# Four additions over all nodes leave GpSimd: bias rows and residual on VectorE, the last two layers' biases as rounded rows in TensorE's sums

## The chip, the core and the metric

The kernel runs on one core of a Trainium2 chip. The metric is the device time in microseconds of one execution, as the median of several; lower is better.

## What is computed

Four graph networks follow each other over 625 nodes with 512 numbers each and 10,000 edges. Each takes the normed and rectified nodes and is added to them:

```python
h = jnp.maximum(_layernorm(x, axis=-1), 0.0)
x = x + L0(h, ...)   # x = h + attention(h) @ Wo + bo;  x + gelu(norm(x) @ W1 + b1) @ W2 + b2
h = jnp.maximum(_layernorm(x, axis=-1), 0.0)
x = x + L1(h, ...)   # edge filters, segment sums
h = jnp.maximum(_layernorm(x, axis=-1), 0.0)
x = x + L2(h, ...)   # three layers: own part and two means over neighbours
h = jnp.maximum(_layernorm(x, axis=-1), 0.0)
x = x + L3(h, ...)   # two layers: agg + x @ root + bias
```

Four of the additions are the matter of the change: the row `bo` on the residual of L0's attention, the row `b2` and the residual on `x`, and the bias rows of L3's two layers (`bias1`, `bias2`).

## The kernel before

Nodes lie in 5 chunks (`NC`) of 128 partitions. `xs` holds x and `hn` the normed nodes, each 128 x 5 x 512 fp32 in SBUF. `rows` holds two rows of 512, spread over all partitions: first `bo` and `b2`, later, loaded into the same place, `bias1` and `bias2`. The program is written out by hand, one instruction stream an engine, with semaphores between them; nothing is scheduled by a planner, so the order in the code is the order on each engine.

The stretches that matter, in order of time:

- **Sorting and V (to 170 us).** GpSimd scatters the edges by 80 indirect DMAs (L736), and then gathers the logits by 84 (L749), while VectorE and ScalarE copy the dense products (L1319). VectorE then adds the row `bv` to V's five chunks (L1325) as TensorE finishes them.
- **Softmax and messages (to 460 us).** VectorE combines L3's basis matrices (`combine_run`), then makes the softmax. GpSimd gathers V for 84 tiles of edges into a ring of 21 (`gather_v`, L758). After the first 21 it adds `bo` to `hn` (L764), then goes on as VectorE frees ring entries.
- **Norm 2 (462 to 500 us).** For each chunk m, TensorE gives the product with Wo, VectorE adds it to `hn[m]` and takes mean and variance (`add_wo`, L1460, then L1281 to L1283), ScalarE the square root (L851), VectorE the factors (L1288, L1289), ScalarE the normed nodes (L856, `s_norm`), TensorE transposes them, ScalarE copies them twice, as rounded upper part `hT_r` and whole `h2_all` (L963, L964), and VectorE subtracts (`rest_of_norm2`, L1467, `s_h2_rest`).
- **FFN1 (to 596 us).** 32 blocks through one PSUM bank, each of 12 fp32r matmuls, emptied by ScalarE with Gelu (L996). Block n of the first chunk half waits for `s_h2_rest` of 3 chunks. From the fifth block on, counting matmuls lie between them.
- **L2 and L3 (from 900 us).** Each fp32 product is three fp32r matmuls: upper x upper, upper x rest, rest x upper (`three`, L2138). A layer is `own` (the nodes' own part into five banks), then for two sides i `side` (products G, emptied by ScalarE twice, L1079 and L1080, and subtracted by VectorE, L1651) and `neighbours` (their sum over the adjacency), which needs all five chunks of G. Meanwhile VectorE combines L3's basis matrices (`combine`, L1675).

GpSimd's queue after the gathers is: wait for norm 2 of all chunks, two additions over all nodes (L768, L769), then the loads for a first combination (`load_lead`, L778). VectorE waits for `s_added` of these before it goes on in FFN1 (L1520) and writes into `hn`. In the last layer (l = 4) GpSimd adds `bias2` to `xs` (L821) between the loads of two weights, and VectorE waits for it before the last additions (L1739). `bias1` is put into `own` of l = 3 by an fp32 matmul of one row:

```python
if l == 3:
    pe.wait_ge(s_l3par, 6 * 16)
    pe.matmul(o, ones[0:1, :], rows[0:1, 0, :], start=True, stop=False)
```

Of the kernel before, what the change touches and what calls it, by code (L numbers as in the profile page):

```python
# [26 lines left out]
ALU = mybir.AluOpType  # L27
# [3 lines left out]
P = 128  # L31
# [64 lines left out]
def seen(turn, m=NC - 1):  # L96

    return sum(NC if t in EACH else 1 for t in range(turn)) + (m + 1 if turn in EACH else 1)
# [81 lines left out]
def build(nc, a, out):  # L180

    with ExitStack() as ctx:
        def sb(name, shape, dt=F32):
            return ctx.enter_context(nc.sbuf_tensor(name, shape, dt))
# [122 lines left out]
        rows = sb("rows", [P, 2, D])  # L307
# [201 lines left out]
        bas_run = [work[:, at:at + 1024] for at in (2048, 3072, 4096)]  # L509
        bas = [aux[:, 8448:9472], aux[:, 9472:10496], wA[:, 6400:7424]]  # L510
# [46 lines left out]
        def _(sp):  # L557
# [45 lines left out]
            for j, count in enumerate((3, 3, 2, 2)):  # L603
                sp.wait_ge(s_pair_out[j], 16 * count)
            sp.dma_start(wo, a["L0_gnn_Wo"].rearrange("(k p) n -> p k n", p=P)).then_inc(s_wo, 16)
# [93 lines left out]
        def _(pool):  # L699
# [61 lines left out]
            gather_v(range(RING))  # L761
            pool.wait_ge(s_norm, seen(1))
            pool.wait_ge(s_wo, 3 * 16)
            pool.tensor_tensor(hn[:, :, :], hn[:, :, :], rows[:, 0, :].unsqueeze(1).to_broadcast([P, NC, D]), ALU.add).then_inc(s_added, 1)  # L764
            gather_v(range(RING, NT))

            pool.wait_ge(s_norm, seen(2))
            step(pool.tensor_tensor(xs[:, :, :], xs[:, :, :], hn[:, :, :], ALU.add))  # L768
            pool.tensor_tensor(xs[:, :, :], xs[:, :, :], rows[:, 1, :].unsqueeze(1).to_broadcast([P, NC, D]), ALU.add).then_inc(s_added, 1)  # L769

# [43 lines left out]
            for l in range(1, LAYERS):  # L814
# [3 lines left out]
                if l == LAYERS - 1:  # L818
                    pool.wait_ge(s_norm, seen(5))
                    pool.wait_ge(s_l3par, 6 * 16)  # L820
                    pool.tensor_tensor(xs[:, :, :], xs[:, :, :], rows[:, 1, :].unsqueeze(1).to_broadcast([P, NC, D]), ALU.add).then_inc(s_added, 1)  # L821
# [333 lines left out]
        def _(dve):  # L1155
# [165 lines left out]
            step(dve.memset(hot[:, NT:NT + 4, :], 0.0))  # L1321
            dve.wait_ge(s_wqkv, 32)
# [125 lines left out]
            dve.wait_ge(s_added, 1)  # L1448
# [9 lines left out]
            def add_wo(m):  # L1458
                dve.wait_ge(s_job, plan.number(f"wo{m}", 0))
                step(dve.tensor_tensor(hn[:, m, :], plan.slot(ps, f"wo{m}", 0), hn[:, m, :], ALU.add))  # L1460
                dve.nop().then_inc(s_by_dve, 1)
                moments(2, m, hn)

# [56 lines left out]
            dve.wait_ge(s_added, 2)  # L1520
# [174 lines left out]
            for l in range(LAYERS):  # L1695
# [21 lines left out]
                if l == 0:  # L1717
                    dve.wait_ge(s_w_upper, 3)
                    dve.tensor_tensor(gws_r[:, 1, :], gw[:, :, :, :].rearrange("p l r k -> p (l r k)"), gws_r[:, 0, :], ALU.subtract)
                rest_of_weight(l, 2)  # L1720
# [18 lines left out]
            dve.wait_ge(s_added, 3)  # L1739
# [5 lines left out]
        def _(pe):  # L1745
# [409 lines left out]
            def own(l, m):  # L2155

                if m == 0:
                    pe.wait_ge(s_w_rest, 3 * l + 1)
                pe.wait_ge(s_rest, 15 * l + m + 1)
                o = ps[:, D * m:D * (m + 1)]  # L2160
                if l == 3:
                    pe.wait_ge(s_l3par, 6 * 16)
                    pe.matmul(o, ones[0:1, :], rows[0:1, 0, :], start=True, stop=False)
                for k in range(K4):
                    last = three(o, h_upper[:, m, cols(k)], h_rest[:, m, cols(k)], w_upper[0][:, k, :], w_rest[0][:, k, :], start=k == 0 and l != 3)
                if m == NC - 1:
                    last.then_inc(s_w_used, 1)
# [98 lines left out]
```

## Time and profile before

| | before |
|---|---|
| median of 3 runs | 1398.02 us (1396.14, 1398.02, 1404.21) |
| the profiled execution, its own time | 1396.14 us |
| its span, first to last instruction | 1394.4 us |
| mean granted TensorE clock | 0.918 of 2.4 GHz |
| TensorE busy | 1173.3 us, 84% |
| VectorE busy | 870.1 us, 62% |
| ScalarE busy | 436.0 us, 31% |
| GpSimd busy | 442.2 us, 32% |

Times in rows are microseconds from the span's start. PE is TensorE's matmul, PEld its weight load, DVE VectorE, ACT ScalarE, POOL GpSimd; L12 is line 12 of the kernel before. An fp32 matmul shows as two records, and a matmul's record is longer than its share of TensorE, since they are pipelined; the distance of starts tells the pace. Idle time in brackets, with what ended it, stands before the instruction that it belongs to.

### The profile page before, as it was taken

How to read it: one execution, taken by the hardware profiler on the slowest of the kernel's cores; microseconds unless marked ns; L12 is line 12 of the kernel's file. 1: busy time of each engine (PE TensorE's matmuls, PEld its weight loads, DVE VectorE, ACT ScalarE, POOL GpSimd, SP SyncE). 2: the span in 40 equal slices, each digit the busy share in tenths (PEclk: the TensorE clock that was granted, in tenths of full speed). 3: DMA queues.
4: the chain of work that ended last, by engine and by line, in shares of the span. 5: the costliest groups of instructions: out<-in, count | busy, mean ns of one | idle time of the engine just before them, and what ended most of it. 6: DMA issues, size and time to landing. Idle time of an engine off the chain costs nothing.

```text
span 1394.4 us, 15192 instructions
## 1 busy us (share of the span) xinstructions
PE 1173.3 (84%) x5432; PEld 822.4 (59%) x5433; DVE 870.1 (62%) x1392; ACT 436.0 (31%) x617; POOL 442.2 (32%) x408
## 2 busy tenths in 40 slices
PE   4597678058798759999997999799799998989996
PEld 4464344033353347744464999567588786778885
DVE  7618326883475557979368997646769877583211
ACT  2315122011211532110053996634232324333220
POOL 5777577783477030111007772000000000010000
PEclk8798889578899979999978999999899999899898
DMA  6216899873766013452016110204645656323001
GB/s 216 45 13 211 278 380 360 277 217 128 242 181 185 17 40 112 136 170 87 31 57 157 49 47 15 91 31 165 206 132 195 206 175 206 108 72 109 0 0 37
DMA packets 74832, 187.83 MB, mean 135 GB/s; under 512 B 14918, under 2 KB 17963, under 8 KB 69524
## 3 DMA queue, kind: packets, MB, share of 16 engines
q1 hardware_dynamic: 45540, 100.35, 21.2%
q0 software_dynamic: 21600, 64.66, 16.1%
q10 hardware_dynamic: 7632, 22.02, 4.2%
q8 instruction: 38, 0.62, 0.2%
q14 instruction: 22, 0.18, 0.0%
HBM read 149.93 MB, written 36.97 MB: 134 GB/s over the span
## 4 chain that ended last, share of the span: by engine, by line
PE 57%; DVE 17%; DMA 10%; issue 6%; ACT 5%; POOL 2%; SPq 2%; DVEq 0%; ACTq 0%; PEldq 0%
PE ps L2138 22%; DMA work<-in_L_gnn_basis 5%; PE ps L2043 5%; PE ps L2101 4%; PE ps L2033 4%; PE ps L1954 4%; DVE aux L1675 3%; PE ps L1810 3%; PE ps L1868 2%; DVE work L1352 2%; PE ps L2013 2%; POOL aux L758 2%; PE ps L1841 2%; PE ps L2086 1%; DMA xs<-in_x 1%
## 5 line engine op out<-in xcount | busy, mean ns | idle before, releaser
L2138 PE MATMUL ps<-work_r,hT_r 128*128 128x512 f32 x600 | 194.8, 406 | 2.1 <-DVE att_r L1647 1.4
L2138 PEld LDWEIGHTS ps<-work_r,hT_r 128*128 128x128 f32 x600 | 114.2, 193 | 32.8 <-issue 4.7
L2138 PE MATMUL ps<-work_r,att_r 128*128 128x512 f32 x300 | 120.8, 403 | 0.0
L736 POOL DMA_INDIRECT etab_d<-aux,edge x80 | 95.2, 1190 | 49.7 <-issue 48.6
L1651 DVE TENSOR_TENSOR bT_r<-bT,fT_r 128x512 fp32r<-128x512 f32 x50 | 38.7, 774 | 107.3 <-ACT fT_r L1080 107.3
L1675 DVE SCALAR_TENSOR_TENSOR aux<-aux,attb 128x1024 f32<-128x1024 f32 x84 | 103.1, 1278 | 2.2 <-DMA aux<-in_L_gnn_basis 2.2
L1810 PE MATMUL ps<-wA 128*128 128x512 f32 x192 | 89.0, 624 | 13.4 <-DMA wA<-in_L_gnn_W_bwd 6.6
L749 POOL DMA_INDIRECT lg<-pair_d,reli x84 | 87.2, 1038 | 29.1 <-issue 25.3
L2138 PE MATMUL ps<-fT_r,wA_r 128*128 128x512 f32 x250 | 87.1, 417 | 10.6 <-DVE bT_r L1651 10.6
L1954 PE MATMUL ps<-work,hT_r 128*128 128x512 f32 x168 | 86.2, 646 | 10.0 <-DVE work L1426 5.7
L1352 DVE SCALAR_TENSOR_TENSOR work<-work,attb 128x1024 f32<-128x1024 f32 x58 | 72.0, 1299 | 28.5 <-DMA work<-in_L_gnn_basis 28.5
L1493 DVE TENSOR_SCALAR work<-iota,srcf,flag 128x640 bf16<-128x640 f16 x168 | 64.4, 448 | 40.6 <-PE ps L2014 40.6
L758 POOL DMA_INDIRECT aux<-v_d,srcx x64 | 80.6, 1260 | 20.0 <-issue 18.0
L2138 PE MATMUL ps<-fT_r,aux_r 128*128 128x512 f32 x250 | 80.8, 401 | 3.6 <-DVE bT_r L1651 3.6
L2101 PE MATMUL ps<-work_r 128*128 128x256 f32 x280 | 70.6, 289 | 9.8 <-DVE wA_r L1581 9.8
L1810 PEld LDWEIGHTS ps<-wA 128*128 128x128 f32 x192 | 37.9, 200 | 61.5 <-issue 51.1
L2043 PE MATMUL ps<-wA,aux 128*128 128x512 f32 x160 | 73.1, 599 | 1.2 <-issue 1.2
L799 POOL DMA_DIRECT2D work<-early_d x9 | 4.9, 544 | 207.8 <-PE ps L2138 135.1
L2101 PE MATMUL ps<-wA_r,work_r 128*128 128x256 f32 x280 | 69.3, 288 | 0.0
L2138 PEld LDWEIGHTS ps<-work_r,att_r 128*128 128x128 f32 x300 | 57.8, 193 | 14.2
L2138 PEld LDWEIGHTS ps<-fT_r,wA_r 128*128 128x128 f32 x250 | 49.2, 197 | 25.9 <-DVE bT_r L1651 12.4
L1426 DVE TENSOR_TENSOR work<-aux,lg 128x512 f32<-128x512 f32 x64 | 44.3, 693 | 28.5 <-DMA aux<-v_d,srcx 16.0
(387 smaller groups left out, 2646.0 us busy)
## 6 DMA issues: line engine op xcount, KB each, us to landing
aux<-in_L_gnn_basis SPq DMA_DIRECT2D x44, 512.0 KB, 3.9
work<-in_L_gnn_basis SPq DMA_DIRECT2D x30, 512.0 KB, 7.6
fT<-in_L_gnn_basis POOLq DMA_DIRECT2D x24, 512.0 KB, 4.4
wA<-in_L_gnn_basis SPq DMA_DIRECT2D x22, 512.0 KB, 3.9
work<-early_d POOLq DMA_DIRECT2D x9, 1024.0 KB, 6.5
wA<-in_L_gnn_W_self ACTq DMA_DIRECT2D x7, 1024.0 KB, 14.9
pair_d<-aux SPq DMA_DIRECT2D x5, 1280.0 KB, 13.7
early_d<-work ACTq DMA_DIRECT2D x5, 1024.0 KB, 17.0
```

What stands on the lines that cost most here:

```text
L736: pool.indirect_dma_start(out=etab_d, out_offset=bass.IndirectOffsetOnAxis(ap=row[:, t:t + 1], axis=0), in_=etab[:, t, :], in_offset=None) ...
L749: pool.indirect_dma_start(out=lg[:, t, :], out_offset=None, in_=pair_d, in_offset=bass.IndirectOffsetOnAxis(ap=reli[:, t:t + 1], axis=0)). ...
L758: pool.indirect_dma_start(out=ring[t % RING], out_offset=None, in_=v_d, in_offset=bass.IndirectOffsetOnAxis(ap=srcx[:, t:t + 1], axis=0)). ...
L1352: ins = dve.scalar_tensor_tensor(acc_run[:, r], bas_run[b % 3], factor, acc_run[:, r], ALU.mult, ALU.add)
L1493: last = dve.tensor_scalar(hotS[:, 4 * k + j, :], iota16[:, :], srcf[:, at], flag[:, r, at], ALU.is_equal, ALU.mult)
L1675: ins = dve.scalar_tensor_tensor(acc[:, r], bas[u], factor, acc[:, r], ALU.mult, ALU.add)
L1810: last = pe.matmul(to[:, k], w[:, o, k * P:(k + 1) * P], early_s[:, o, :], start=o == 0, stop=o == K4 - 1)
L1954: pe.matmul(ps[:, bass.ds(c * 512, D)], one, msg[:, j, :], start=False, stop=False, skip_group_check=True)\
L2033: last = pe.matmul(o, w, h[:, k, nodes], start=k == i == 0, stop=(k, i) == (K4 - 1, 2))
L2043: last = pe.matmul(plan.slot(ps, "ffn2", m), node(g1T, j, m), w2s[:, j, :], start=j == 0, stop=j == 15)
L2101: last = pe.matmul(ps[:, 512 * m:512 * m + NF], hotL[k][:, j, m * P:(m + 1) * P], part[:, 4 * k + j, :], start=False, stop=False)
L2138: last = pe.matmul(o, lhsT, rhs, start=start and n == 0, stop=stop and n == 2)
```

## The change

On GpSimd the four additions go, and with them the waits ahead of them. `bo` and `b2` are now added by VectorE, both over all nodes, behind the copies of the dense products and before the additions to V. The residual `xs += hn` is split into five, one behind each chunk's `moments` in `add_wo`. `bias1` and `bias2` become two-partition fp32r rows, the rounded row and what it lacks, made once by VectorE in layer 0; TensorE adds them in `own` of l = 3 and l = 4 with one fp32r matmul of two rows each. SP's one added wait is met long before.

```diff
-        rows = sb("rows", [P, 2, D])
+        rows, rows_r = sb_twice("rows", [P, 2, D])
...
+        bias_upper = wA_r[0:2, 7424:7424 + D]
+        ones_r = wA_r[0:2, 7936:7936 + P]
...
+            sp.wait_ge(s_wo, 32)
             sp.dma_start(wo, a["L0_gnn_Wo"].rearrange("(k p) n -> p k n", p=P)).then_inc(s_wo, 16)
...
-            gather_v(range(RING))
-            pool.wait_ge(s_norm, seen(1))
-            pool.wait_ge(s_wo, 3 * 16)
-            pool.tensor_tensor(hn[:, :, :], hn[:, :, :], rows[:, 0, :].unsqueeze(1).to_broadcast([P, NC, D]), ALU.add).then_inc(s_added, 1)
-            gather_v(range(RING, NT))
-
+            gather_v(range(NT))
             pool.wait_ge(s_norm, seen(2))
-            step(pool.tensor_tensor(xs[:, :, :], xs[:, :, :], hn[:, :, :], ALU.add))
-            pool.tensor_tensor(xs[:, :, :], xs[:, :, :], rows[:, 1, :].unsqueeze(1).to_broadcast([P, NC, D]), ALU.add).then_inc(s_added, 1)
...
-                if l == LAYERS - 1:
-                    pool.wait_ge(s_norm, seen(5))
-                    pool.wait_ge(s_l3par, 6 * 16)
-                    pool.tensor_tensor(xs[:, :, :], xs[:, :, :], rows[:, 1, :].unsqueeze(1).to_broadcast([P, NC, D]), ALU.add).then_inc(s_added, 1)
...
             step(dve.memset(hot[:, NT:NT + 4, :], 0.0))
+            dve.wait_ge(s_wo, 32)
+            dve.wait_ge(s_norm, seen(1))
+            for j, nodes in enumerate((hn, xs)):
+                dve.tensor_tensor(nodes[:, :, :], nodes[:, :, :], rows[:, j, :].unsqueeze(1).to_broadcast([P, NC, D]), ALU.add).then_inc(s_added, 1)
...
-            dve.wait_ge(s_added, 1)
+            dve.wait_ge(s_added, 2)
...
                 moments(2, m, hn)
+                dve.tensor_tensor(xs[:, m, :], xs[:, m, :], hn[:, m, :], ALU.add).then_inc(s_added, 1)
...
-            dve.wait_ge(s_added, 2)
+            dve.wait_ge(s_added, 2 + NC)
...
+                    dve.wait_ge(s_l3par, 6 * 16)
+                    step(dve.tensor_copy(ones_r, ones[0:2, :]))
+                    for j in range(2):
+                        step(dve.tensor_copy(bias_upper, rows[0:2, j, :]))
+                        step(dve.tensor_tensor(rows_r[0:2, j, :], rows[0:2, j, :], bias_upper, ALU.subtract))
+                        step(dve.tensor_copy(rows_r[0:1, j, :], bias_upper[0:1]))
...
-            dve.wait_ge(s_added, 3)
...
-                if l == 3:
-                    pe.wait_ge(s_l3par, 6 * 16)
-                    pe.matmul(o, ones[0:1, :], rows[0:1, 0, :], start=True, stop=False)
+                if l >= 3:
+                    pe.matmul(o, ones_r, rows_r[0:2, l - 3, :], start=True, stop=False)
                 for k in range(K4):
-                    last = three(o, h_upper[:, m, cols(k)], h_rest[:, m, cols(k)], w_upper[0][:, k, :], w_rest[0][:, k, :], start=k == 0 and l != 3)
+                    last = three(o, h_upper[:, m, cols(k)], h_rest[:, m, cols(k)], w_upper[0][:, k, :], w_rest[0][:, k, :], start=k == 0 and l < 3)
```

On VectorE, between the clearing of the last four tiles of `hot` and the additions to V (`aux<-ps,wA`), the order before is:

```order
148 L1321 MEMSET work 128x256
149 L1325 TENSOR_TENSOR aux<-ps,wA 128x512 [waits s_pre_job,s_wqkv,s_dve]
150 L1325 TENSOR_TENSOR aux<-ps,wA 128x512 [waits s_pre_job] x4
151 L1330 CAST srcx<-att 128x28 [waits s_att0]
152 L1331 CAST dstx<-att 128x28
```

and now:

```order
148 L1312 MEMSET work 128x256
149 L1316 TENSOR_TENSOR hn<-hn,rows 128x2560 [waits s_norm,s_wo,s_dve]
150 L1316 TENSOR_TENSOR xs<-xs,rows 128x2560
151 L1320 TENSOR_TENSOR aux<-ps,wA 128x512 [waits s_pre_job,s_wqkv]
152 L1320 TENSOR_TENSOR aux<-ps,wA 128x512 [waits s_pre_job] x4
```

The two additions over all nodes stand ahead of the first addition to V.

On VectorE in norm 2, for chunk 1 and the beginning of chunk 2, the order before is (the subtraction into `wA_r` is that of a W1 block):

```order
363 L1460 TENSOR_TENSOR hn<-ps,hn 128x512 [waits s_job]
364 L1281 BN_STATS bst<-hn 128x6 [waits s_dve]
365 L1282 BN_AGGR mv<-bst 128x2 [waits s_dve]
366 L1283 TENSOR_SCALAR var<-mv 128x1 [waits s_dve]
367 L1288 RECIPROCAL rstd<-std 128x1 [waits s_std]
368 L1289 SCALAR_TENSOR_TENSOR nmr<-mv,rstd 128x1 [waits s_dve]
369 L1444 TENSOR_TENSOR wA_r<-wA,work_r 128x512 [waits s_w1_upper]
370 L1460 TENSOR_TENSOR hn<-ps,hn 128x512 [waits s_job]
```

and now:

```order
366 L1455 TENSOR_TENSOR hn<-ps,hn 128x512 [waits s_job]
367 L1272 BN_STATS bst<-hn 128x6 [waits s_dve]
368 L1273 BN_AGGR mv<-bst 128x2 [waits s_dve]
369 L1274 TENSOR_SCALAR var<-mv 128x1 [waits s_dve]
370 L1458 TENSOR_TENSOR xs<-xs,hn 128x512
371 L1279 RECIPROCAL rstd<-std 128x1 [waits s_std]
372 L1280 SCALAR_TENSOR_TENSOR nmr<-mv,rstd 128x1 [waits s_dve]
373 L1439 TENSOR_TENSOR wA_r<-wA,work_r 128x512 [waits s_w1_upper]
```

The addition to `xs` stands between the variance and the reciprocal that waits for the square root.

On GpSimd in the last layers, the order before is (`work<-rel_d` are the weights of the two sides, the one ahead of them the own weight):

```order
182 L799 DMA work<-in_L3_gnn_root2 128x4x512 [waits s_w_used]
183 L821 TENSOR_TENSOR xs<-xs,rows 128x2560 [waits s_l3par,s_norm,s_job]
184 L799 DMA work<-rel_d 128x2048 [waits s_rel_out]
185 L799 DMA work<-rel_d 128x2048 [waits s_job]
```

and now:

```order
178 L823 DMA wA<-adj_d 128x3200 [waits s_job]
179 L794 DMA work<-in_L3_gnn_root2 128x4x512 [waits s_w_used]
180 L794 DMA work<-rel_d 128x2048 [waits s_rel_out,s_job]
181 L794 DMA work<-rel_d 128x2048 [waits s_job]
182 L182 UNCONDITIONAL_BRANCH
```

The addition is gone, and the load behind it keeps its wait for the job of side 0.

## Rows read from the trace of the kernel before

**Rows 1.** The page's head.

```profile
span 1394.4 us, 15192 instructions
```

**Rows 2.** GpSimd's additions by line: ns min/median/max, first and last start.

```profile
L764 POOL TENSOR_TENSOR hn<-hn,rows x1: 5600/5600/5600, 319.8 to 319.8; 128x2560 f32<-128x2560 f32 x1
L768 POOL TENSOR_TENSOR xs<-xs,hn x1: 5711/5711/5711, 488.9 to 488.9; 128x2560 f32<-128x2560 f32 x1
L821 POOL TENSOR_TENSOR xs<-xs,rows x1: 5675/5675/5675, 1235.4 to 1235.4; 128x2560 f32<-128x2560 f32 x1
```

**Rows 3.** L1467 by line, and its last four in VectorE's timeline (start, duration).

```profile
L1467 DVE TENSOR_TENSOR bT_r<-bT,hT_r x5: 677/685/6068, 483.8 to 501.6; 128x512 fp32r<-128x512 f32 x5
...
489.08 13.25 DVE L1467 TENSOR_TENSOR bT_r<-bT,hT_r 128x512 fp32r<-128x512 f32 x4
```

**Rows 4.** The chain that ended last, around FFN1's start: start, us, what.

```profile
489.97 11.25 issue
501.23 3.55 PE ps L2033 x12
...
505.48 3.55 PE ps L2033 x12
```

**Rows 5.** Timelines of VectorE and TensorE in layer 3's first side.

```profile
1236.63 4.97 DVE L1651 TENSOR_TENSOR bT_r<-bT,fT_r 128x512 fp32r<-128x512 f32 x1 [1.51 <-ACT fT_r L1080]
...
1241.66 0.50 PE L2138 MATMUL ps<-fT_r,aux_r 128*128 128x512 f32 x1 [3.59 <-DVE bT_r L1651]
```

**Rows 6.** Waits from 320 to 462 us: who waited, total, times, longest.

```profile
DVE bT L1416 <- PE ps L1917: 24.6, 1, 24.6
```

**Rows 7.** ScalarE's timeline at FFN1's start.

```profile
494.93 1.28 ACT L996 ACT_TABLE_LOAD   x1
```

**Rows 8.** Windows: length, busy us of each engine, PEclk, DMA share, GB/s.

```profile
501.20:505.40 4.20, 3.54 (x12) 3.16 (x12) 4.20 (x11) 0.53 (x1) 0.88 (x2) 0.50 0.73 250
...
509.60:512.30 2.70, 2.01 (x12) 1.77 (x12) 0.00 (x0) 0.53 (x1) 0.00 (x0) 1.00 0.00 0
```

**Rows 9.** ScalarE's timeline in norm 2, chunk 1.

```profile
474.60 0.82 ACT L856 ACTIVATE aux<-hn,nmr,rstd 128x512 f32<-128x512 f32 x1 [0.42 <-DVE nmr L1289]
```

**Rows 10.** Around V, and a long addition and a held gather elsewhere.

```profile
152.80 0.69 DVE L1325 TENSOR_TENSOR aux<-ps,wA 128x512 f32<-128x512 f32 x1 [5.51 <-PE ps L1895]
...
159.53 1.20 POOL L736 DMA_INDIRECT etab_d<-aux,edge  x1 [7.51 <-issue]
...
L1643 DVE TENSOR_TENSOR wA_r<-wA,wA_r x2: 3477/3484/3492, 962.3 to 1241.5; 128x3200 fp32r<-128x3200 f32 x2
...
301.35 4.79 POOL L758 DMA_INDIRECT aux<-v_d,srcx  x1 [0.30 <-issue]
```

**Rows 11.** Gathers of logits: by line, DMA landing (us), and their first use.

```profile
L749 POOL DMA_INDIRECT lg<-pair_d,reli x84: 940/945/1738, 169.6 to 281.2; - x84
...
lg<-pair_d,reli POOLq DMA_INDIRECT x84, 5.5
...
288.80 0.86 DVE L1366 SCALAR_TENSOR_TENSOR lg<-lg,att 128x672 f32<-128x672 f32 x1
```

**Rows 12.** VectorE's timeline in layer 0, around the place of the conversions.

```profile
943.88 3.49 DVE L1714 TENSOR_TENSOR aux_r<-aux,aux_r 128x3200 fp32r<-128x3200 f32 x1 [13.53 <-ACT aux_r L1124]
...
953.93 0.69 DVE L1651 TENSOR_TENSOR bT_r<-bT,fT_r 128x512 fp32r<-128x512 f32 x1 [2.12 <-ACT fT_r L1080]
```

**Rows 13.** Layer 3's own product: TensorE's timeline, and ScalarE's.

```profile
1188.46 1.12 PE L2163 MATMUL ps<-rows,ones 1*128 1x512 f32 x2
1189.51 0.73 PE L2138 MATMUL ps<-work_r,hT_r 128*128 128x512 f32 x2
...
1191.53 0.81 ACT L856 ACTIVATE hn<-xs,nmr,rstd 128x512 f32<-128x512 f32 x1 [2.16 <-DVE nmr L1289]
```

**Rows 14.** Windows behind L1651's wait, columns as in rows 8.

```profile
1241.60:1246.60 5.00, 4.94 (x15) 3.91 (x16) 5.00 (x3) 0.00 (x0) 0.00 (x0) 0.66 0.00 0
1246.60:1260.00 13.40, 13.40 (x59) 10.85 (x58) 13.40 (x12) 0.00 (x0) 0.00 (x0) 1.00 0.37 119
```

## The prediction

> **What bounds the kernel now.** I began with the page. The span is 1394.4 us [rows 1], the profiled execution took 1396.14 us, so 1.7 us lie around the span. No engine is busy all of it, so a change is worth what it does at the waits that end last. The changed instructions are therefore read one by one in time order, first those that go, then those that come.
>
> GpSimd's four additions take 5.6 to 5.9 us each; the row of the second also stands for the third, which follows it directly [rows 2]. The reader is to look at what VectorE and TensorE do meanwhile, not at GpSimd, whose own time is cheap. In the groups of one line, the VectorE subtraction L1467 (fp32r of 128x512) has a median of 0.685 us and a maximum of 6.07 us; four of them, started at 489.08, occupied 13.25 us [rows 3]. 13.25 less four times 0.685 is 10.5 us too much, and it lies inside the time of the two additions on `xs` (488.9 to 500.6). The two long L1467 end some 0.5 us behind the two additions (the first addition at 494.6), and what they read had been ready before. So a GpSimd addition that reads SBUF holds back a VectorE instruction with two SBUF inputs until it ends. The chain of waits shows who pays: TensorE stands for 11.25 us until 501.23, when the subtraction for nodes 2 is done and FFN1's first block may begin; the second block begins at 505.48 [rows 4].
>
> The fourth addition does the same at 1235.4: one L1651 takes 4.97 us, and TensorE stands 3.59 us for it before the fifth part of `neighbours(3, 0, 0)` [rows 5]. The first addition, at 319.8, lies under a stretch in which VectorE later waits 24.6 us for TensorE anyway [rows 6].
>
> **The change part by part.**
>
> *The two additions after norm 2 go.* The subtraction for nodes 2 is then done at about 490.7 (489.08, plus two of 0.6 to 0.7 us, plus the 0.3 us below), and FFN1's first block starts there instead of at 501.23. It uses the one bank that the second block needs too, and ScalarE empties it only after its table load, which starts at 494.93 and takes 1.28 us [rows 7]: 496.2, plus 0.3, plus 0.53 us of eviction and 0.14 us to the start give 497.2 for the second block. Against 505.48 that is 8.3 us. The bound then is ScalarE, so the 10.5 us do not all come back. TensorE's clock takes some of it away. Before, the first two blocks run at a granted 0.50 and take 4.2 us each with their gap; the third, at 1.00, takes 2.7 [rows 8]. After, the first slow block lies under ScalarE's work, a gap of some 2.9 us follows it, and the third may be slow as well: 4.2 less 2.7 is 1.5 us. I find no row that says which, so the term is 7.6 us, between 6.8 and 8.3. What follows, FFN1 to the last layer, is paced by its own predecessors and moves as a block; GpSimd's loads for the combination, issued behind the additions at 500.6, go out earlier, but VectorE first uses them some ten FFN1 blocks later, so that buys nothing.
>
> *Five small additions come* (`xs[m] += hn[m]`, 128x512, 0.69 us each) in VectorE's norm 2 part. Each is issued between the variance and the reciprocal that waits for ScalarE's square root. For nodes 1 that gap is some 0.4 us, and ScalarE itself had 0.42 us idle before its next instruction at 474.60 [rows 9]: the reciprocal is late by 0.3 us, and ScalarE is the path from there on. For nodes 2 to 4 ScalarE has copies to make first, and the wait is longer than the addition. Cost 0.3 us, already in the 497.2; the bounds are 0 and, with no cover at all, 5 x 0.69 = 3.5 us.
>
> *Two large additions come* (128x2560) on VectorE before the additions to V. VectorE stands 5.51 us before L1325 at 152.80 [rows 10]. L1643 does 128x3200 from two SBUF inputs in 3.48 us; with 0.685 for 128x512 the slope is 1.04 ns an element, so 2560 elements take 2.8 us, two of them 5.6 us. They fill the gap to within 0.1 us, and the next L1325 is 3.3 us later: cost 0. The other side of it is GpSimd, which is issuing scatters then. A gather that met L1359 (3.9 us, two SBUF inputs) took 4.79 us instead of 0.95 [rows 10]. So the two additions may delay the scatters by about 3 us. The rows show GpSimd's next pause, 7.51 us before 159.53 [rows 10]. It begins at 152.0, where the delay would end, and no engine is named as its cause; if it hangs on an event outside, it swallows the delay, and I take that, cost 0. If it does not, the gathers of logits end 3 us later: the last starts at 281.2 and lands 5.5 us on, 286.7, against the 288.80 at which VectorE uses them [rows 11]. Slack 2.1 us, so at most 1 us is left on the path, 3 us if the landing is already the limit.
>
> The Trainium skill (SBUF — State Buffer, Who interferes with whom) says that a `tensor_tensor` with two SBUF inputs blocks GpSimd instructions that read SBUF, whichever came first, and by inference not the writing of DMA descriptors. By that rule these scatters would not be held at all and the term is 0 in any case. The 4.79 us speak against the second half; the 6.07 us agree with the first.
>
> *The bias rows.* Rounding them adds seven small VectorE instructions of two partitions in layer 0, by the 0.69 us of 128x512 at most 4.3 us. They stand before the subtraction for the third weight. VectorE stood 13.53 us before the instruction ahead of them and stands 2.1 us before the L1651 that follow [rows 12]; the fourth is on time again, and TensorE needs all five. Cost 0, at most 4.3.
>
> In layer 3 the fp32 matmul with one row took 1.05 us of TensorE (1188.46 to the next at 1189.51) [rows 13]. An fp32r of 512 columns at full clock takes 0.23 us: 59 in 13.40 us [rows 14]. Saving 0.82 us for each of five, but the first is lost, since the transposition behind it waits for ScalarE's L856 (1191.53 plus 0.81, 1192.3) [rows 13] and was there only 0.1 us later before. 4 x 0.82 + 0.1 = 3.4 us. Layer 4 gains five such instructions: 5 x 0.23 = 1.2 us lost. Net 2.2 us gained, with bounds of 0 (the rows of layer 3 wait for VectorE's `h_rest` instead) and 2.9.
>
> *The last addition goes.* TensorE's 3.59 us vanish, since the last L1651 then ends 0.7 us after its start, before TensorE is there. And the granted clock, 1.00 before and after, is 0.66 over the 5.0 us behind the stand [rows 14]: 5.0 x 0.34 = 1.7 us more. I take 5.2 us (3.6 to 5.3). VectorE's next, L1643, must then wait for ScalarE's L1143 until 1239.4, so VectorE gains less than TensorE; its stretch to the first L1651 of the second side may end some 2 us late, and the third of the five is on time again. The wait for the final `s_added` and the DMA behind the addition on GpSimd's queue were not waited for: 0.
>
> *Sum:* 7.6 + 5.2 + 2.2 = 15.0 us off the 1396.1 us of the profiled execution, 1381.1. That execution is the fastest of the three, 1.9 us under their median of 1398.0, and the slowest is 8 above it; I leave the sum as it is, and take the spread into the range.
>
> **The rivals.** 0.5%, about what a measurement of this kernel tells from no change, is 7.0 us.
>
> *Forecast* (0.80): both stands of TensorE go, 1377 to 1385.
>
> *The early additions are paid* (0.09): GpSimd's scatters are late by more than the pause covers. For it: 4.79 us against 0.95. Against: the pause and 2.1 us of slack. 1 to 3 us: 1382 to 1384, and 1386 if V is late too.
>
> *The long L1467 has another cause* (0.08), say ScalarE's copies or a port that the five new additions hit as well; then only the bias rows are left, 1396.1 - 2.2 + 0.3 = 1394. Against it: both long instructions end with a GpSimd addition, and so does L1651's. The Trainium skill (the same section) calls this an exclusive lock for the whole instruction, which the rows bear out.
>
> *Slower than before* (0.03): the clock. With a gap in the middle of FFN1's start, TensorE could stay at 1.2 GHz for further blocks, 1.5 us each. After 10 such blocks the 15.0 us are gone, after 15 it is 7 us slower: 1403. Against it: from the fifth block on counting matmuls fill the gaps, and the rows show 1.00 from the third [rows 8].
>
> **How the numbers follow.** The likeliest gives 1381. Its lower side is 8.3 + 5.3 + 2.9 = 16.5 and no more, 1379.6; with the executions' spread 1376. Its upper side 6.8 + 3.6 + 0 less 3 for the scatters is 7.4, 1388.7. The range 1376 to 1389 holds the first two cases, 0.89 less what the spread of medians takes. Faster 0.89, same 0.08, slower 0.03.
>
> **What would show it.** No L1467 or L1651 over 1 us. FFN1's first block at about 490.7 and the second at 497.2 (if that one is at 501 or later, the first term is wrong), the third at 0.50 or 1.00. The stretch at 147 to 153 full on VectorE, scatters of 3 us beside it, and the logits used at 288.8 as before. The own product of layer 3 with 0.23 us rows; no stand before `neighbours(3, 0, 0)`'s last part, and no drop of the clock behind it. The forecast fails if another engine ends the two waits a little later.

## The result, and the profile after

The change makes the kernel faster by 0.9%: the median of 12 runs is 1383.62 us against 1393.46 us of the kernel before in the same comparison, and the ratio of the runs is 0.9911, with a 95% interval of 0.9883 to 0.9940. Of 1393.46 us that is 12.4 us (8.4 to 16.3); the two medians themselves lie 9.8 us apart, inside that interval. The forecast was 15.0 us against one execution and a time of 1381.1 us. A second comparison (s0_change below) gave 1382.51 us and a ratio of 0.9897 (0.9862 to 0.9932), 14.4 us.

The profiled execution of the changed kernel took 1392.82 us, the longest of its twelve. It shows only 3.4 us less than the profiled execution of before, so its parts have to be read one by one. First the page's head, which answers to [rows 1], and its engine line:

```profile
span 1391.0 us, 15181 instructions
PE 1173.7 (84%) x5414; PEld 823.3 (59%) x5433; DVE 861.5 (62%) x1406; ACT 436.0 (31%) x617; POOL 421.1 (30%) x404
```

**Norm 2 and FFN1.** VectorE's subtraction by line (ns min/median/max) answers to [rows 3], TensorE's timeline to [rows 4], ScalarE's to [rows 7]:

```profile
L1463 DVE TENSOR_TENSOR bT_r<-bT,hT_r x5: 683/686/693, 493.2 to 503.9; 128x512 fp32r<-128x512 f32 x5
...
499.93 0.61 PE L2034 MATMUL ps<-hT_r,work_r 128*128 128x320 f32 x1 [0.95 <-issue]
...
506.35 0.61 PE L2034 MATMUL ps<-hT_r,work_r 128*128 128x320 f32 x1 [2.88 <-ACT aux L987]
...
504.38 1.28 ACT L987 ACT_TABLE_LOAD   x1
```

No subtraction takes 6 us any more, and TensorE stands 0.95 us ahead of FFN1's first block instead of 11.25. The second block waits for ScalarE, as forecast. Counted from the first addition of Wo's product to `hn` (467.76 before, 477.00 here), the first block comes 10.5 us and the second 8.4 us earlier.

**Layers 3 and 4.** TensorE's timeline in layer 3's own product [rows 13], VectorE's around the place of the last addition [rows 5], and windows behind it (length, PE busy, PEclk, DMA share, GB/s) [rows 14]:

```profile
1188.33 0.50 PE L2163 MATMUL ps<-rows_r,wA_r 2*128 2x512 f32 x1
1188.76 0.74 PE L2139 MATMUL ps<-work_r,hT_r 128*128 128x512 f32 x2
...
1192.26 0.66 PE L2153 MATMUL ps<-ident,hn 128*128 128x128 f32 x4 [0.43 <-ACT hn L847]
```

And in layer 4, where there was no row before, from the last transposition to the first small matmul of the gates, which is three parts of `own`, before and after:

```profile
1296.78 0.60 PE L2152 MATMUL ps<-ident,hn 128*128 128x128 f32 x4
...
1305.64 0.28 PE L2138 MATMUL ps<-gws_r,hT_r 128*128 128x2 f32 x2
```

```profile
1291.57 0.60 PE L2153 MATMUL ps<-ident,hn 128*128 128x128 f32 x4
...
1302.30 0.28 PE L2139 MATMUL ps<-gws_r,hT_r 128*128 128x2 f32 x2
```

```profile
1235.54 0.69 DVE L1647 TENSOR_TENSOR bT_r<-bT,fT_r 128x512 fp32r<-128x512 f32 x1 [1.51 <-ACT fT_r L1071]
1238.31 3.49 DVE L1639 TENSOR_TENSOR wA_r<-wA,wA_r 128x3200 fp32r<-128x3200 f32 x1 [2.08 <-ACT wA_r L1134]
```

```profile
1233.00:1241.00 8.00, 8.00 (x36) 1.00 0.24 89
1241.00:1247.00 6.00, 6.00 (x27) 1.00 0.00 0
```

From a bias row to the next matmul it is 0.43 us, not the 0.23 us forecast (1.05 before). Its whole price is higher still, since the matmuls beside it are spaced wider too: in layer 4 three parts take 10.73 us with rows and 8.86 us without, 0.62 us a row. In layer 3 TensorE waits 0.43 us for ScalarE ahead of the second transposition, where the first row's gain is lost, as forecast. The stand of 3.59 us and the clock of 0.66 behind it are gone.

**What is worse.** Around V, VectorE's and GpSimd's timelines answer to [rows 10]:

```profile
147.86 2.82 DVE L1316 TENSOR_TENSOR hn<-hn,rows 128x2560 f32<-128x2560 f32 x1
150.60 2.82 DVE L1316 TENSOR_TENSOR xs<-xs,rows 128x2560 f32<-128x2560 f32 x1
153.34 0.68 DVE L1320 TENSOR_TENSOR aux<-ps,wA 128x512 f32<-128x512 f32 x1
```

```profile
148.27 3.47 POOL L739 DMA_INDIRECT etab_d<-aux,edge  x1 [0.31 <-issue]
152.04 2.44 POOL L739 DMA_INDIRECT etab_d<-aux,edge  x1 [0.30 <-issue]
154.78 1.18 POOL L739 DMA_INDIRECT etab_d<-aux,edge  x1 [0.30 <-issue]
163.03 1.20 POOL L739 DMA_INDIRECT etab_d<-aux,edge  x1 [7.07 <-issue]
```

The additions take 2.8 us each and fit into VectorE's gap, but two scatters beside them take 3.47 and 2.44 us instead of 1.19, and GpSimd's pause did not swallow it: 7.07 us instead of 7.51, and the scatter behind it is 3.5 us later than before. The edges' rows land at 175.2 instead of 168.3, VectorE's combination of basis matrices starts 7.3 us later and the softmax's first copy 6.8 us later (296.53 against 289.69). One block of TensorE's early products, in whose first third the granted clock is 0.50 (16.80 us at 346.56, against 13.97 us before), adds 2.8 us more; by the first addition of Wo this execution is 9.2 us behind that of before. The experiments ask first whether this is the change or the execution.

### The profile page after: what moved, and what is told of

It reads as the page before. It is cut to its first block, busy times and chain, and to the rows that moved or that the text cites. A ratio compares the mean times of both kernels' runs of the same rounds, so it can differ in the third digit from the quotient of the medians.

```text
span 1391.0 us, 15181 instructions
## 1 busy us (share of the span) xinstructions
PE 1173.7 (84%) x5414; PEld 823.3 (59%) x5433; DVE 861.5 (62%) x1406; ACT 436.0 (31%) x617; POOL 421.1 (30%) x404
## 3 DMA queue, kind: packets, MB, share of 16 engines
q0 software_dynamic: 21600, 64.66, 15.8%
## 4 chain that ended last, share of the span: by engine, by line
PE 58%; DVE 16%; DMA 10%; ACT 5%; issue 5%; POOL 2%; SPq 2%; DVEq 0%; ACTq 0%; PEldq 0%
PE ps L2139 24%; DMA work<-in_L_gnn_basis 6%; PE ps L2044 5%; PE ps L2102 4%; PE ps L1955 4%; PE ps L2034 4%; PE ps L1811 3%; DVE aux L1671 3%; PE ps L1869 2%; DVE work L1347 2%; PE ps L2014 2%; POOL aux L761 2%; DMA pair_d<-aux 2%; PE ps L1842 2%; DMA xs<-in_x 1%
## 5 line engine op out<-in xcount | busy, mean ns | idle before, releaser
L739 POOL DMA_INDIRECT etab_d<-aux,edge x80 | 98.8, 1235 | 50.9 <-issue 50.0
L1811 PE MATMUL ps<-wA 128*128 128x512 f32 x192 | 94.1, 653 | 17.4 <-DMA wA<-in_L_gnn_W_fwd 6.2
L1647 DVE TENSOR_TENSOR bT_r<-bT,fT_r 128x512 fp32r<-128x512 f32 x50 | 34.2, 689 | 102.2 <-ACT fT_r L1071 102.1
L1347 DVE SCALAR_TENSOR_TENSOR work<-work,attb 128x1024 f32<-128x1024 f32 x58 | 71.9, 1301 | 28.0 <-DMA work<-in_L_gnn_basis 28.0
L790 POOL DMA_INDIRECT fT<-u_d,dstx x36 | 40.8, 1134 | 77.0 <-DMA u_d<-bT 66.3
## 6 DMA issues: line engine op xcount, KB each, us to landing
wA<-in_L_gnn_W_self ACTq DMA_DIRECT2D x7, 1024.0 KB, 10.5
pair_d<-aux SPq DMA_DIRECT2D x5, 1280.0 KB, 14.2
```

The lines of the kernel that those rows point to most:

```text
L739: pool.indirect_dma_start(out=etab_d, out_offset=bass.IndirectOffsetOnAxis(ap=row[:, t:t + 1], axis=0), in_=etab[:, t, :], in_offset=None) ...
L1347: ins = dve.scalar_tensor_tensor(acc_run[:, r], bas_run[b % 3], factor, acc_run[:, r], ALU.mult, ALU.add)
L1811: last = pe.matmul(to[:, k], w[:, o, k * P:(k + 1) * P], early_s[:, o, :], start=o == 0, stop=o == K4 - 1)
```

## The experiments

Twelve kernels ran in three sets, each set with the kernel before on its own chip. In the first and the third set the kernel before took 1509.56 and 1508.31 us instead of some 1396. TensorE's timeline in the changed kernel there, and VectorE's behind it, tell where:

```profile
265.56 1.01 PE L1811 MATMUL ps<-wA 128*128 128x512 f32 x1 [1.79 <-issue]
268.36 1.01 PE L1811 MATMUL ps<-wA 128*128 128x512 f32 x1 [1.79 <-issue]
270.46 1.01 PE L1811 MATMUL ps<-wA 128*128 128x512 f32 x1 [1.09 <-issue]
...
347.66 0.70 DVE L1368 MEMSET work<- 112x769 f32 x1 [58.94 <-ACT work L919]
```

Here TensorE shows one matmul in 2.1 to 3.5 us from 244 to 316 us, with no releaser for the waits, and VectorE then stands 58.94 us; in r1_late such a stretch lies at 200 to 233 us. Whatever is late on VectorE or GpSimd ahead of 347 us is hidden there. So these two sets say nothing about the additions at 147 us through their times; their rows for single instructions, and for everything behind Wo, still count.

**The changed kernel (r0_change, s0_change).** The same program again.

> The changed kernel once more, beside the three that follow. Theory A: two of GpSimd's scatters are held by VectorE's two early additions, the attribute rows of the edges come 7 us late, and this lasts to the first message. Theory B: the 7 us are the chance of one execution. Both expect a ratio to the kernel before of about 0.991 (12 us less). A: the two scatters take about 3.5 and 2.4 us again and VectorE's first L1341 starts at about 194; B: the scatters are held too, but L1341 starts at 187 to 190 as often as at 194.

Measured: 0.9849 (0.9799 to 0.9899). Two scatters were held again (the longest 3.49 us), the combination started at 189.5, in theory B's range.

> The changed kernel again, for a second set on one chip; in the first set TensorE issued its instructions slowly between 200 and 320 us (one matmul in about 2.8 us), which hid what stood ahead of 347 us. If this set shows TensorE at its usual pace there, theory A expects 0.991 and L1341 at about 194; if it is slow again, 0.985 to 0.991 as in the first set.

Measured, with TensorE at its usual pace: 1382.51 us, 0.9897 (0.9862 to 0.9932). GpSimd's timeline:

```profile
146.57 3.84 POOL L739 DMA_INDIRECT etab_d<-aux,edge  x1 [0.30 <-issue]
150.72 2.43 POOL L739 DMA_INDIRECT etab_d<-aux,edge  x1 [0.30 <-issue]
...
161.10 1.20 POOL L739 DMA_INDIRECT etab_d<-aux,edge  x1 [4.96 <-issue]
```

The same two scatters were held, 3.9 us together; this time the pause behind them shrank to 4.96 us, and the next scatter was 1.8 us late (against 159.26 in the late version below). The combination started at 188.6, so the 194 of the first profile did not come back.

**The additions of rows moved to a wait (r1_late, s1_late).**

```diff
-            dve.wait_ge(s_wo, 32)
-            dve.wait_ge(s_norm, seen(1))
-            for j, nodes in enumerate((hn, xs)):
-                dve.tensor_tensor(nodes[:, :, :], nodes[:, :, :], rows[:, j, :].unsqueeze(1).to_broadcast([P, NC, D]), ALU.add).then_inc(s_added, 1)
...
             dve.tensor_tensor(aT[:, :], fwd[:, :], bwd[:, :], ALU.max).then_inc(s_soft, 1)
+            dve.wait_ge(s_wo, 32)
+            dve.wait_ge(s_norm, seen(1))
+            for j, nodes in enumerate((hn, xs)):
+                dve.tensor_tensor(nodes[:, :, :], nodes[:, :, :], rows[:, j, :].unsqueeze(1).to_broadcast([P, NC, D]), ALU.add).then_inc(s_added, 1)
```

> The two additions of rows over all nodes stand in VectorE's wait of 24 to 29 us ahead of L1411 instead of before the additions to V. Theory A: all scatters take 1.19 us, L1341 starts at about 187, the softmax's copies at about 290, and the time is 5 to 7 us under the change's, ratio to the kernel before 0.986 to 0.988. Theory B: the same time as the change within 2 us. Both: VectorE's wait ahead of L1411 is shorter by 5.6 us and nothing is later for it.

Measured: 1502.03 us, 0.9928 (0.9896 to 0.9960), on a chip that hides the place.

> The two additions of rows in VectorE's wait ahead of L1411, in the second set. At TensorE's usual pace theory A expects 5 to 7 us under the change (0.986 to 0.988), theory B no difference of more than 2 us. With TensorE slow between 200 and 320 us both expect no difference.

Measured: 1381.32 us, 0.9903 (0.9870 to 0.9937), beside 1382.51 us and 0.9897 of the change. Theory A, 5 to 7 us less than the change, is not borne out; theory B's "within 2 us" is what was measured, with intervals of 5 us to either side. GpSimd's scatters by line show what the move did, and it brought no time that can be measured:

```profile
L739 POOL DMA_INDIRECT etab_d<-aux,edge x80: 1182/1187/1425, 32.3 to 160.8; - x80
```

**The additions between those to V (r2_between).** One stands behind V's chunk 1, one behind chunk 2.

> The two additions stand behind V's additions of chunks 1 and 2, where GpSimd makes its pause of 7 us and VectorE waits 2.7 us for TensorE. Theory A, that it is the overlap with scatters that costs: no scatter is held, the additions to V are late by at most 0.3 us, and the time is that of the late version within 2 us. Rival A2, that anything early on VectorE costs by making V and its store late: 2 us or more over the late version. Theory B: like all the others.

Measured: 1496.82 us, 0.9913 (0.9880 to 0.9947), on the hiding chip of r1_late. The pause did not cover both additions: one scatter, at 160.68, still took 2.83 us.

**The additions as scalar_tensor_tensor (r3_early_stt).**

```diff
-                dve.tensor_tensor(nodes[:, :, :], nodes[:, :, :], rows[:, j, :].unsqueeze(1).to_broadcast([P, NC, D]), ALU.add).then_inc(s_added, 1)
+                dve.scalar_tensor_tensor(nodes[:, :, :], nodes[:, :, :], 1.0, rows[:, j, :].unsqueeze(1).to_broadcast([P, NC, D]), ALU.mult, ALU.add).then_inc(s_added, 1)
```

> The two additions stand where the change has them, but as scalar_tensor_tensor (times 1.0, plus the row), 3.1 us each by L1347's 1.28 us for 1024 elements. L1347 has two SBUF inputs too, and the gathers beside it took 0.945 us, as alone. Theory C: only tensor_tensor holds GpSimd's indirect DMAs, so the scatters take 1.19 us and the time is that of the late version within 2 us. Theory D: any VectorE instruction with two SBUF inputs holds them; the scatters take 3 to 4 us and the time is the change's or 1 us more.

Measured: 1493.91 us, 0.9859 (0.9815 to 0.9903), on the same chip. VectorE's and GpSimd's timelines:

```profile
146.28 2.83 DVE L1316 SCALAR_TENSOR_TENSOR hn<-hn,rows 128x2560 f32<-128x2560 f32 x1
```

```profile
146.52 3.64 POOL L739 DMA_INDIRECT etab_d<-aux,edge  x1 [0.30 <-issue]
150.47 2.43 POOL L739 DMA_INDIRECT etab_d<-aux,edge  x1 [0.30 <-issue]
```

The scatters are held as long as by tensor_tensor. Theory C falls, and theory D holds. The gathers of logits beside L1347, a scalar_tensor_tensor of 128x1024 with two SBUF inputs, seem to speak against it, for they keep a median of 0.947 us in this trace. The median hides the answer; VectorE's and GpSimd's timelines show it:

```profile
203.81 4.91 DVE L1347 SCALAR_TENSOR_TENSOR work<-work,attb 128x1024 f32<-128x1024 f32 x4 [2.11 <-issue]
```

```profile
204.14 1.78 POOL L752 DMA_INDIRECT lg<-pair_d,reli  x1 [0.30 <-issue]
206.22 0.94 POOL L752 DMA_INDIRECT lg<-pair_d,reli  x1 [0.30 <-issue]
```

The first of the four L1347 ends at 205.10. The gather that starts 0.33 us into it takes 1.78 us and ends 0.82 us behind that end. In all fourteen traces 101 gathers start 0.1 to 1.1 us into an L1347, and every one ends 0.80 to 0.83 us behind its end. The 561 that start within 0.1 us of its start take 0.95 us at most, and so do those that start in its last 0.1 us; most fall on these two places, which makes the median. The nine held scatters end 1.05 to 1.07 us behind their addition's end. So an indirect DMA of GpSimd is held until VectorE's instruction with two SBUF inputs ends. One thing stays open: in s0_change a scatter that started 0.04 us behind its addition was held in full, where gathers so close to the start are not.

A plain DMA issued by GpSimd is not held. Beside L1710, a tensor_tensor of 3.49 us with two SBUF inputs that starts at 944.05, the first profile of the change shows:

```profile
944.26 0.70 POOL L808 DMA_DIRECT2D aux<-rel_d  x1 [23.26 <-DVEq L1709]
944.96 0.53 POOL L794 DMA_DIRECT2D work<-early_d  x1
```

These two take as long in all fourteen traces (0.70 to 0.71 and 0.53 to 0.55 us).

In this first set the versions with early additions came out lower than those with late ones, 0.9849 and 0.9859 against 0.9928 and 0.9913, against every theory above. The first message stands at 410.2 and 418.3 us in their traces against 423.8 and 430.3, so most of it arises in or behind TensorE's slow stretch. The second set, at the usual pace, did not repeat it; the cause stays open.

**L0 alone (s2_l0_only).** The kernel before with the edits of L0, the two large additions in the later wait; L821 and the fp32 row stay.

> The kernel before, with the three additions of L0 moved as in the change, but the two over all nodes in VectorE's wait ahead of L1411; L3's bias stays an fp32 row of TensorE and a GpSimd addition. Theory: the stand ahead of FFN1 (11.25 us before) is 1 us and the second block comes 8.4 us earlier; 8.6 us in all, ratio 0.994. Rival: GpSimd's loads that go out 10 us earlier collide or the clock stays low, and less than 4 us is left, 0.997 or more.

Measured: 1390.14 us, 0.9944 (0.9922 to 0.9966), 7.8 us (4.7 to 10.9), near the 8.6 us expected.

**L3's rows alone (s3_rows_only).** The kernel before with the other half: rounded rows in `own` of both layers, no L821.

> The kernel before, with L3's two biases as rounded rows in TensorE's sums and without the last GpSimd addition; L0 as before. Theory, from the two traces: 5.4 us for the stand and the low clock behind it, 1.9 us for layer 3's rows, less 1.3 us for layer 4's: 6.0 us, ratio 0.9957. Rival: the low clock that follows each layer's gates moves and takes the gain, 3 us or less, 0.998.

Measured: 1394.16 us, 0.9970 (0.9943 to 0.9997), 4.2 us (0.4 to 8.0), against 6.0 us expected and 3 us or less by the rival, which the interval does not separate. The two halves add up to 12.0 us, within the interval of the whole's 14.4 us in the same set. Their subtractions by line, of s3_rows_only first and of s2_l0_only then, show that each lock goes with its own addition:

```profile
L1465 DVE TENSOR_TENSOR bT_r<-bT,hT_r x5: 679/684/6070, 487.5 to 505.4; 128x512 fp32r<-128x512 f32 x5
...
L1649 DVE TENSOR_TENSOR bT_r<-bT,fT_r x50: 682/689/694, 957.5 to 1363.6; 128x512 fp32r<-128x512 f32 x50
```

```profile
L1467 DVE TENSOR_TENSOR bT_r<-bT,hT_r x5: 682/685/693, 488.5 to 499.2; 128x512 fp32r<-128x512 f32 x5
...
L1651 DVE TENSOR_TENSOR bT_r<-bT,fT_r x50: 673/688/4970, 944.1 to 1360.8; 128x512 fp32r<-128x512 f32 x50
```

**GpSimd busy, but not reading (t2_gp_memset), and with shorter additions (t3_gp_add).** On the late version, behind norm 2. `lg` is not read any more there. First t2's edit, then t3's:

```diff
             pool.wait_ge(s_norm, seen(2))
+            for _ in range(8):
+                step(pool.memset(lg[:, :, :], 0.0))
```

```diff
             pool.wait_ge(s_norm, seen(2))
+            for _ in range(8):
+                step(pool.tensor_tensor(lg[:, :, :], lg[:, :, :], lg[:, :, :], ALU.add))
```

> The late version, with eight memsets of 128x672 on GpSimd behind norm 2, where the two additions stood before. They write SBUF and read none. Theory: VectorE's L1463 beside them take 0.69 us as without, and FFN1's first block stands where it stood. Rival, that a busy GpSimd as such holds VectorE: they take as long as a memset.

> The late version, with eight additions of 128x672 (lg + lg, both inputs in SBUF) on GpSimd behind norm 2, by the 5.7 us for 128x2560 some 1.5 us each, 12 us in all, and shorter ones than before. Theory: each VectorE L1463 that meets one ends with it, so they take up to 1.5 us each more, and FFN1's first block is late by 1 to 3 us, not by 10: what counts is the length of one GpSimd instruction. Rival: VectorE gets no turn between them and the third L1463 ends some 12 us later, as before the change.

Measured, GpSimd's and VectorE's timelines, t2 first:

```profile
561.92 5.67 POOL L767 MEMSET lg<- 128x672 f32 x8 [47.58 <-ACT aux L849]
...
562.14 1.29 DVE L1465 TENSOR_TENSOR bT_r<-bT,hT_r 128x512 fp32r<-128x512 f32 x2
```

```profile
564.13 12.77 POOL L767 TENSOR_TENSOR lg<-lg 128x672 f32<-128x672 f32 x8 [48.96 <-ACT aux L849]
...
564.32 6.93 DVE L1465 TENSOR_TENSOR bT_r<-bT,hT_r 128x512 fp32r<-128x512 f32 x4
```

Beside the memsets two subtractions take 1.29 us, as they do with GpSimd at rest. Beside the additions four take 6.93 us, 1.7 us each, which is about the 1.6 us of one of GpSimd's eight. VectorE gets its turn between them, and FFN1's first block is only 2.2 us late (25.2 us behind the first addition of Wo against 22.9), not 10; the second, which waits for ScalarE, is on time (29.4). Both expectations of the theory hold, each in one execution. A memset here is as short as a subtraction, so t2 rules out a lock over many instructions better than one over a single one.

**Scatters held on purpose (t1_held).** On the late version, four `pool.memset(att[:, :], 0.0)` ahead of scatter 72.

> The late version, with four memsets of 128x3024 on GpSimd ahead of the last eight scatters, which makes these scatters late by the length of the memsets (8 to 16 us, against 1.9 to 3.5 us by the change's two additions). Theory A: the attribute rows land as much later, VectorE's combination starts later, and of each us most is left at the first message (361 without). Theory B: the combination is paced by its DMAs and takes the lateness up; the first message is late by less than a quarter of it.

Measured: 0.9893 (0.9842 to 0.9945), on a hiding chip. The memsets took 10.67 us, GpSimd's pause shrank from about 7.4 to 2.48 us, and the last scatter stood at 166.64 instead of 160.9 to 161.7. The combination started 1.3 to 2.4 us later than in the four other late versions on such chips, and the softmax's copies at 292.54 instead of 278.5 to 282.2. The edges' rows landed at 181.1 instead of 168.0 to 168.9, so of some 13 us only 1.3 to 2.4 reach the combination, while the softmax, for which the gathers of logits must be done, gets 10 us or more. The first message, at 421.52, lies amid the 417.5 to 423.8 of the other four, so neither theory on it is settled; what the lateness costs on a chip that does not hide it was not seen.

**TensorE's gaps filled (t0_fill).** On the late version, bf16 matmuls of no use into a free bank.

```diff
+            def fill(some):
+                for _ in range(some):
+                    pe.matmul(ps[:, 0:512], hot[:, NT, :], hot[:, 0:4, :].rearrange("p t d -> p (t d)"), start=True, stop=True)
...
+            fill(3)
             turn_norm2(3)
+            fill(13)
             turn_norm2(4)
...
+                if n < AHEAD:
+                    fill((3, 16, 3, 3)[n])
```

> The late version, with bf16 matmuls of no use (128x512, into a bank that is free) in TensorE's four gaps around FFN1's start: 3 and 13 ahead of the transposes of nodes 3 and 4, then 3, 16, 3 and 3 ahead of FFN1's first four blocks. In the profiles so far the granted clock fell to 0.50 for 10.2 us or for 20.5 us there, and the fourth block began 13.2 or 14.9 us after the first. Theory: the gaps make the clock fall; with them filled the clock stays at 1.00, the second block still waits for ScalarE, the fifth begins at 14.6 us after the first instead of 16.3 or 19.9, 2 to 5 us off the late version: ratio to before 0.987. Rival: the filling is late by itself or does not hold the clock: the ratio of the late version, 0.990, or more.

Measured: 1494.38 us, 0.9911 (0.9875 to 0.9947), no different from the late version in time; the 0.987 expected lies just outside. Windows of TensorE around FFN1's first block, of the first profile of the change, of the change in the second set, and of t0_fill:

```profile
489.00:499.00 10.00, 5.56 (x24) 1.00 0.00 1
499.00:509.00 10.00, 6.19 (x22) 0.50 0.31 106
509.00:517.00 8.00, 6.51 (x39) 0.98 0.00 0
```

```profile
484.00:494.00 10.00, 5.57 (x23) 0.99 0.00 0
494.00:504.00 10.00, 6.61 (x24) 0.50 0.31 107
504.00:514.00 10.00, 8.58 (x30) 0.50 0.00 0
```

```profile
557.00:567.00 10.00, 8.98 (x38) 1.00 0.00 1
567.00:577.00 10.00, 8.63 (x46) 1.00 0.30 106
```

The clock stays at 1.00, 2.4 GHz, and FFN1's fifth block begins 15.05 us behind the first, against 16.3 or 19.8 to 20.1 us without filling. So the gaps make the clock fall, shown in this one execution against ten without filling; the first and the second block are as early as without it (22.94 and 29.38 us behind the first addition of Wo), so the filling is not late by itself. Its 1 to 5 us are within what the times can't tell apart.

## Why the prediction was right

Times of the same events in the traces of the chips with the usual pace, in us (each taken from the instruction's start):

| | before | change, first | change, second | late | L0 only | rows only |
|---|---|---|---|---|---|---|
| last scatter | 161.03 | 164.53 | 162.61 | 160.76 | 160.93 | 160.83 |
| combination starts | 186.72 | 194.01 | 188.56 | 186.73 | 186.80 | 186.73 |
| softmax's first copy | 289.69 | 296.53 | 293.57 | 294.94 | 292.82 | 292.52 |
| first message | 360.03 | 369.61 | 364.14 | 361.30 | 362.08 | 361.39 |
| Wo's first addition to FFN1's fifth block | 47.86 | 39.27 | 42.77 | 42.77 | 42.95 | 47.86 |
| layer 3, fifth to tenth L1651 | 36.87 | 31.48 | 31.48 | 31.48 | 36.88 | 31.46 |
| layer 3, first `h_rest` to the gates' first matmul | 22.68 | 20.14 | 20.15 | 20.15 | 22.67 | 20.16 |
| from there to the first L1651 | 15.87 | 17.46 | 14.24 | 14.21 | 15.88 | 15.83 |
| tenth L1651 to the first matmul of layer 4's gates | 32.14 | 35.28 | 35.30 | 35.28 | 32.15 | 35.31 |
| from there to the first L1651 | 17.44 | 17.45 | 14.22 | 14.23 | 17.45 | 14.21 |

*FFN1's start (7.6 us, 6.8 to 8.3).* The place, the waits and the 8.3 us at the second block were right: 8.4, with the block 29.35 us behind the first addition of Wo where the forecast has 29.4. What follows has two values, 8.6 us or 5.1 us. The granted clock falls to 0.50 (1.2 GHz) around the gaps ahead of the first block. Of the ten traces with L0 changed and nothing added in this place (all but t0_fill, t3_gp_add and s3_rows_only), it came back after 10.2 us in four, late in the second block, so that the third is fast, and after 20.5 us in six, with four slow blocks; both kinds stand in the windows of t0_fill's section. The forecast named "the third may be slow as well", for 1.5 us; it did not see that a fourth comes with it. Before, the low stretch was 20.5 us too, but began 12.5 us ahead of the first block, in the stand, and ended with the second block; now it begins 0.9 to 1.8 us ahead of it. The mean over the ten is about 6.5 us.

*Five small additions (0.3 us) and conversions (0).* Counted from the first addition of Wo, the first two subtractions start 0.2 us later than before (16.2 and 21.5 us against 16.0 and 21.3), as forecast; the third, no longer held up, starts at 22.14 to 22.17 us against 27.31, in all traces with L0 changed but t3_gp_add. In layer 0 the seven conversions take 3.5 us (the forecast's bound of 4.3 should be 4.8, seven times 0.69). Counted from the layer's fifth `h_rest`, the first L1651 is late by that, 23.4 us against 19.9, and the fifth is on time, 29.9 in both profiles.

*The last addition (5.2 us).* 5.4 us in every trace without it, with nothing in the way.

*The bias rows (2.2 us).* This term was mis-sized, and without the clock it has the wrong sign. The forecast priced a row at 0.23 us, the pace of a matmul in a long run of them; a row costs 0.62 us. Layer 3 therefore gains 2.5 us up to its gates, not 3.4 us, and layer 4 loses 3.1 us, not 1.2 us, in every one of the twelve traces with rows: 0.6 us lost. Then comes the clock. Over each layer's gates, matmuls of two columns, it is low for 6.8, 10.2 or 13.7 us, and from the gates to the first L1651 it takes 14.2, 15.8 or 17.5 us in layer 3 and 14.2 or 17.4 us in layer 4. The kernel before and s2_l0_only both show 15.9 and 17.4; the means of the twelve are 15.7 and 15.5. That gives back 0.2 and 1.9 us, so the net term is 1.5 us of gain, and that it lies near the forecast's 2.2 is luck. Whether the kernel without rows varies here too, its two traces can't tell.

*The early additions (0, rival 1 to 3 us).* That the scatters would be held by some 3 us was right. That the pause swallows it was wrong: of 3.5 us and 3.9 us added, 3.5 and 1.8 us came through it. In the first profile that was followed by a combination 7.3 us later. There the edges' rows were loaded from `etab_d` by an issue at 167.66, behind SP's burst of loads from 166.77 on, instead of at 164.16, ahead of it; they were used 6.9 us later, and the chain of waits stands 21.1 us for the first basis matrix. That the two loads got into each other's way fits these times and was not tried alone. It can't be all: in r0_change the rows' load was issued behind SP's burst too and landed at 172.2, in t1_held it landed at 181.1, and the combination started at 189.5 and 189.3. What made it 194.0 in the first profile stays open. In the second profile the combination started 1.8 us late, and at the softmax's first copy the lateness was gone: 293.57 stands amid the 292.5 to 294.9 of the three kernels without early additions. The combination waits 28 to 34 us for its DMAs, and these set its end. The medians differ by 1.2 us, change against late version, with intervals of 5 us to either side. So the cost is 0 to 7 us in an execution, and no more than about 1 us is seen in the medians; whether the 7.3 us of one execution are rare was not settled.

*The sum.* 6.5, 5.4 and 1.5 are 13.4 us, less something for the early additions; measured were 12.4 and 14.4. The two large terms rest on their mechanisms. The small one erred in the price of a row, 2.8 us in all, and the clock gave 2.1 of it back. Between FFN1's last block and layer 3 the traces scatter from 588.2 to 596.0 us, whatever the kernel, so that a term of 1 or 2 us in that stretch could not be seen.

## What to carry to other kernels

A GpSimd addition is priced by what VectorE has to do meanwhile: look for VectorE instructions far over their median, and see whose end theirs coincides with. If such work must stay on GpSimd, short instructions cost far less than one long one. The other way round, a VectorE instruction with two SBUF inputs holds GpSimd's indirect DMAs; here that cost 3.5 to 3.9 us of GpSimd's time. An instruction that is squeezed in between matmuls is priced by the distance of the blocks around it (0.62 us), not by the pace of a long run (0.23). And where a stand of TensorE is removed, ask at which clock the work behind it now starts: the gain at the first instruction (10.5 us) shrinks at the next engine's table load (8.4) and again at the clock (5.1 or 8.6).

## What was not expected of the hardware

- The granted clock behind the same gap was low for 10.2 us or for 20.5 us, with the same program and the same waits, which makes 3.5 us between executions at this one place.
- Indirect DMAs of GpSimd wait for the end of a VectorE instruction with two SBUF inputs, in tensor_tensor and scalar_tensor_tensor alike: 101 gathers ended 0.80 to 0.83 us behind it, nine scatters 1.05 to 1.07 us. Plain DMAs issued by GpSimd did not wait. A median over all gathers shows none of it.
- An fp32r matmul of two partitions by 512 columns, put between matmuls of 128 by 512, cost 0.62 us, where these follow each other in 0.23 us.
- On the chips of two of the three sets TensorE showed stretches of single matmuls, mostly 2.8 us apart, with no releaser; the whole kernel took 8% longer there. The cause stays open.
